# Recurrent stage: the candidate's input share enters its PSUM bank by a product of TensorE

## The chip, the core and the metric

The kernel runs on one core of a Trainium2 chip. The metric is the device time of one execution, in microseconds (us). TensorE appears in the profile as PE (products) and PEld (weight loads), VectorE as DVE, ScalarE as ACT, GpSimd as POOL; a "q" behind an engine's name is its sequencer.

## The reference, cut to what matters

The program is a chain of eight residual blocks over x (8 batches of 256 tokens, 128 features). The third is the recurrent one that the change touches. It walks over the 256 tokens of all 8 batches at once, one step a token, and each step needs the state of the step before:

```
def step(h, x_t):                                  # h: 8 x 128
    score = tanh([h, enc] @ W_att) @ V_att         # enc: 64 context rows of each batch
    attn = softmax(score)
    context = attn @ enc
    gz, gr, gh = split([x_t, context] @ Wi + b)    # input share + context share
    rz, rr, rh = split(h @ Uh)                     # state share
    z, r = sigmoid(gz + rz), sigmoid(gr + rr)
    hh = tanh(gh + r * rh)                         # the candidate
    return z * h + (1 - z) * hh
x = x + the states of all steps
```

The other seven blocks (slot attention, top heads, switch experts, six transformer layers, a top-2 block, a gated block, a quantised linear one) stand before and behind it and are not changed.

## The kernel before, in words

`attentive_gru` (from L1018) has three parts. A preparation makes the input shares `x_t @ Wi + b` of all steps and gates (tile `gx`, gates 0 = z, 1 = r, 2 = candidate) and the context rows times `Wi` (`encw`). Then a hardware loop runs four passes of 64 unrolled steps (L1145, `STEPS_A_PASS`), with a barrier of all engines between passes. A last part adds the states to x.

The order of work is written out by hand for each engine, and semaphores tie the engines together; a wait is named after what it waits for. A step goes round the engines like this. TensorE forms the query (L1185 with the kept part `zh`, L1188 with the new part `part`), VectorE adds it to the encoded context (L1270, two halves), ScalarE takes tanh (L1237, `th`), TensorE makes the scores (L1200), VectorE their minimum (L1274), ScalarE the exponentials (L1239), TensorE turns them (L1209), VectorE copies them (L1278), TensorE makes the three context shares (L1163), VectorE and ScalarE copy these out (L1283, L1241, L1285; `crows`), TensorE turns and adds them into the gates' banks (`turn_part`, L1171), ScalarE takes the gates' tanh (L1244 for r, L1246 for z; a sigmoid is written as half of 1 + tanh), VectorE forms `u` (L1288), `gh` (L1290), `u2` (L1293), `zh` (L1298) and `omz` (L1300), ScalarE the candidate (L1248), VectorE `part` (L1302), and GpSimd the new state (L1255, L1258).

PSUM banks: 0 the query, 5 the r gate, 4 the z gate, 7 the candidate's state share, 6 the candidate's context share, 3 a bank that is never read. Banks 5 and 4 are opened by `input_part` (L1168, an identity product that writes the input share), take the state share (L1194, L1195) and are closed by `turn_part`. Bank 6 is written by `turn_part` alone, and VectorE adds the input share (`gh`).

`keep_busy` (L1157) issues products of a zero tile into the unread bank 3, of 128 to 512 columns. They stand between the real products in TensorE's queue, so that it always has something to do. A step has 13 of them, two of 448 columns before the first wait for `tanh_ready`.

Of the kernel before, what the change touches and what calls it, by code (L numbers as in the profile page):

```python
# [7 lines left out]
ALU = mybir.AluOpType  # L8
# [8 lines left out]
P = 128  # L17
D = 128
B, S = 8, 256
# [998 lines left out]
def attentive_gru(nc, dram, X, psum, cst):  # L1018


    with ExitStack() as ctx:
        def sb(name, shape, dt=F32):
            return ctx.enter_context(nc.sbuf_tensor("g1_" + name, shape, dt))
# [19 lines left out]
        attn, attnT, shares = sb("attn", [P, C]), sb("attnT", [P, B + 32]), sb("shares", [P, B])  # L1043
        crows = sb("crows", [P, 3, D])
        wa_half = sb("wa_half", [P, D])
        gh, kept, tr, tz, u, u2, cand, omz, zh, part = (sb(n, [P, B]) for n in ("gh", "kept", "tr", "tz", "u", "u2", "cand", "omz", "zh", "part"))
        still = sb("still", [P, 512], BF16)

        with engines_pass(nc) as (block, sig):
            @block.sync  # L1050
            def _(sp):
                for dst, src in ((wa, "G1_wa"), (wi, "G1_wi"), (ctxT, "ctxT"), (uh, "G1_uh"), (bias, "G1_bias"),
                                 (vcol, "G1_v"), (pick, "c_pick")):
                    sp.dma_start(dst[:], dram[src]).then_inc(sig["loads"], 16)
                sp.dma_start(h[:, 0, :], dram["embT"]).then_inc(sig["loads"], 16)
# [89 lines left out]
        with nc.Fori(0, S // STEPS_A_PASS) as group:  # L1145


            with engines_pass(nc) as (block, sig):
                def gx(gate, s):
                    return GX[:, gate, :, ds(group * STEPS_A_PASS + s, 1)].rearrange("p b a -> p (b a)")  # L1150

                @block.tensor
                def _(pe):
                    def keep_busy(bank, cols, n=1):

                        for _ in range(n):
                            pe.matmul(psum[:, bank, 0:cols], cst["ident_bf"][:], still[:, 0:cols], start=True, stop=True)  # L1157

                    def context_part(gate, bank, ready):


                        for p in range(PAIRS):
                            last = pe.matmul(psum[32 * p:32 * p + 32, bank, 0:D], attnT[:, 2 * p:2 * p + 32],  # L1163
                                             encw[:, p, gate, :], start=True, stop=True)
                        last.then_inc(sig[ready], 1)

                    def input_part(gate, bank, s):
                        pe.matmul(psum[:, bank, 0:B], cst["ident"][:], gx(gate, s), start=True, stop=False)  # L1168

                    def turn_part(i, bank, ready, start=False):  # L1170
                        pe.matmul(psum[:, bank, 0:B], crows[:, i, :], shares[:], start=start, stop=True)\  # L1171
                          .then_inc(sig[ready], 1)

                    keep_busy(3, 512, 18)
                    input_part(1, 5, 0)
                    input_part(0, 4, 0)
                    for s in range(STEPS_A_PASS):
                        hs = h[:, s % 2, :]

                        if s == 0:  # L1180
                            pe.matmul(psum[:, 0, 0:B], wa[:, 0, :], hs, start=True, stop=True)\
                                .then_inc(sig["query_ready"], 1)
                        else:
                            pe.wait_ge(sig["kept_part_ready"], s)
                            pe.matmul(psum[:, 0, 0:B], wa_half[:], zh[:], start=True, stop=False)  # L1185
                            keep_busy(3, 256)
                            pe.wait_ge(sig["new_part_ready"], s)
                            pe.matmul(psum[:, 0, 0:B], wa[:, 0, :], part[:], start=False, stop=True)\  # L1188
                                .then_inc(sig["query_ready"], 1)
                            keep_busy(3, 256)  # L1190
                            pe.wait_ge(sig["state_ready"], s)
                        pe.matmul(psum[:, 7, 0:B], uh[:, 2, :], hs, start=True, stop=True)\
                          .then_inc(sig["state_products_ready"], 1)
                        pe.matmul(psum[:, 5, 0:B], uh[:, 1, :], hs, start=False, stop=False)  # L1194
                        pe.matmul(psum[:, 4, 0:B], uh[:, 0, :], hs, start=False, stop=False)  # L1195
                        keep_busy(3, 448, 2)
                        for i in range(2):
                            pe.wait_ge(sig["tanh_ready"], 2 * s + i + 1)
                            for p in range(PAIRS):
                                last = pe.matmul(psum[32 * p:32 * p + 32, 1, 0:C], vneg[:, i, :], th[:, i, p, :],  # L1200
                                                 start=i == 0, stop=i == 1)
                            if i == 0:
                                keep_busy(3, 320)
                        last.then_inc(sig["scores_ready"], 1)
                        keep_busy(3, 512, 3)

                        pe.wait_ge(sig["exp_ready"], s + 1)
                        for i in range(2):
                            last = pe.matmul(psum[C * i:C * i + C, 2, 0:B], attn[:], pick[:, i, :], start=True, stop=True)  # L1209
                        last.then_inc(sig["attn_turned"], 1)  # L1210
                        keep_busy(3, 384, 2)
                        pe.wait_ge(sig["attnT_ready"], s + 1)
                        context_part(1, 3, "context_r_ready")
                        context_part(2, 1, "context_h_ready")
                        context_part(0, 2, "context_z_ready")
                        pe.wait_ge(sig["shares_ready"], s + 1)
                        pe.wait_ge(sig["context_r_taken"], s + 1)
                        turn_part(0, 5, "gate_r_ready")
                        pe.wait_ge(sig["context_h_taken"], s + 1)
                        turn_part(1, 6, "context_h_turned", start=True)  # L1220
                        keep_busy(3, 192)
                        pe.wait_ge(sig["context_z_taken"], s + 1)
                        turn_part(2, 4, "gate_z_ready")
                        keep_busy(3, 512)
                        if s + 1 < STEPS_A_PASS:
                            pe.wait_ge(sig["tanh_r_ready"], s + 1)
                            input_part(1, 5, s + 1)
                            keep_busy(3, 128)
                            pe.wait_ge(sig["tanh_z_ready"], s + 1)
                            input_part(0, 4, s + 1)  # L1230
# [32 lines left out]
                def _(dve):  # L1263
                    steps = Steps(dve, sig["vector_steps"])

                    for s in range(STEPS_A_PASS):
                        dve.wait_ge(sig["query_ready"], s + 1)
                        query = psum[:, 0, 0:B].rearrange("p (b i) -> p i b", i=2)
                        for i in range(2):
# [16 lines left out]
                        dve.wait_ge(sig["tanh_r_ready"], s + 1)  # L1286
                        dve.wait_ge(sig["state_products_ready"], s + 1)
                        dve.scalar_tensor_tensor(u[:], tr[:], 1.0, psum[:, 7, 0:B], ALU.add, ALU.mult).then_inc(sig["reset_ready"], 1)  # L1288
                        dve.wait_ge(sig["context_h_turned"], s + 1)
                        dve.tensor_tensor(gh[:], psum[:, 6, 0:B], gx(2, s), ALU.add).then_inc(sig["candidate_part_ready"], 1)  # L1290
                        dve.wait_ge(sig["reset_ready"], s + 1)
                        dve.wait_ge(sig["candidate_part_ready"], s + 1)
                        dve.scalar_tensor_tensor(u2[:], u[:], 0.5, gh[:], ALU.mult, ALU.add)\  # L1293
                            .then_inc(sig["candidate_input_ready"], 1)
                        dve.wait_ge(sig["tanh_z_ready"], s + 1)
                        if s >= 1:
# [2338 lines left out]


PHASES = [slot_attention, top_heads, attentive_gru, switch_experts, dit_layers, top2_block, glu_block, ternary_linear]


# [126 lines left out]
```

## Time and profile before

| | us |
|---|---|
| median of 3 runs | 5760.1 |
| lowest, highest | 5753.37, 5780.07 |
| the profiled execution's own time | 5762.91 |
| its span, from the first to the last instruction | 5761.1 |
| busy: PE 4907.7 (85%), DVE 2920.8 (51%), ACT 2109.4 (37%), POOL 585.3 (10%) | |
| the steps of the recurrent stage | from about 446 to 2235 |

Busy time is a sum over instructions. In the recurrent stage most of what PE does is `keep_busy` (the costliest group of the page, 1018.9 us), so a busy PE doesn't mean that PE sets the time there. "PEclk" is the granted TensorE clock as a share of its upper level: 1.00 is 2.4 GHz, 0.50 is 1.2 GHz.

### The profile page before, as it was taken

How to read it: one execution, taken by the hardware profiler on the slowest of the kernel's cores; microseconds unless marked ns; L12 is line 12 of the kernel's file. 1: busy time of each engine (PE TensorE's matmuls, PEld its weight loads, DVE VectorE, ACT ScalarE, POOL GpSimd, SP SyncE). 2: the span in 40 equal slices, each digit the busy share in tenths (PEclk: the TensorE clock that was granted, in tenths of full speed). 3: DMA queues.
4: the chain of work that ended last, by engine and by line, in shares of the span. 5: the costliest groups of instructions: out<-in, count | busy, mean ns of one | idle time of the engine just before them, and what ended most of it. 6: DMA issues, size and time to landing. Idle time of an engine off the chain costs nothing. (4 is left out here: it accounts for less than half of the span.)

```text
span 5761.1 us, 115322 instructions
## 1 busy us (share of the span) xinstructions
PE 4907.7 (85%) x46515; PEld 3114.7 (54%) x46515; DVE 2920.8 (51%) x9818; ACT 2109.4 (37%) x4155; POOL 585.3 (10%) x1312
## 2 busy tenths in 40 slices
PE   4389999999999996588989888898869897788784
PEld 3256666666666664355545555455534574555563
DVE  5634444444444443477666777677636323334343
ACT  2223222222222221166656666566534332122221
POOL 3300000000000002211111111111110000000000
PEclk7689899898998997699999999999979798898896
DMA  0010000000000001100000000000000001000000
GB/s 24 7 32 2 2 2 2 2 2 2 2 2 2 2 2 50 54 6 4 9 4 9 4 5 5 7 8 4 6 38 1 1 1 41 1 1 1 1 1 9
DMA packets 33174, 51.08 MB, mean 9 GB/s; under 512 B 8596, under 2 KB 24118, under 8 KB 32000
## 3 DMA queue, kind: packets, MB, share of 16 engines
q1 hardware_dynamic: 29312, 39.67, 2.1%
q8 instruction: 383, 6.28, 0.4%
q10 hardware_dynamic: 2304, 2.11, 0.1%
q0 software_dynamic: 1024, 1.78, 0.1%
q14 instruction: 151, 1.24, 0.1%
HBM read 39.03 MB, written 4.19 MB: 8 GB/s over the span
## 5 line engine op out<-in xcount | busy, mean ns | idle before, releaser
L1157 PE MATMUL psum<-g_still,ident_bf 128*128 128x512 bf16 (+6 forms) x3388 | 1018.9, 359 | 19.1 <-issue 17.5
L2277 DVE TENSOR_REDUCE l_m<-psum 128x2 bf16<-128x512 f32 x768 | 503.8, 693 | 164.8 <-PE psum L1881 161.7
L1157 PEld LDWEIGHTS psum<-g_still,ident_bf 128*128 128x128 bf16 x3388 | 409.1, 139 | 144.1 <-issue 84.6
L2153 ACT ACTIVATE l_probs<-psum,l_mcol 128x1024 f32<-128x1024 f32 x384 | 406.7, 1110 | 175.5 <-PE psum L1919 175.5
L1881 PE MATMUL psum<-l_kb,l_qmb 32*128 32x256 bf16 x1536 | 299.0, 276 | 70.6 <-DVE l_m L2277 52.0
L1237 ACT ACTIVATE g_th<-g_pre 128x256 f32<-128x256 f32 x512 | 192.2, 418 | 348.8 <-DVE g_pre L1270 348.8
L1919 PE MATMUL psum<-l_qm,l_keys 32*128 32x256 f32 x3072 | 268.3, 422 | 14.6 <-issue 14.6
L1270 DVE TENSOR_TENSOR g_pre<-g_encp,psum 128x256 f32<-128x256 f32 x512 | 192.9, 418 | 168.4 <-PE psum L1188 120.9
L2164 ACT COPY l_heads_out<-psum 128x256 f32<-128x256 f32 (+1 forms) x292 | 130.3, 446 | 367.6 <-PE psum L1945 184.8
L1945 PE MATMUL psum<-l_probs,l_v 128*32 128x256 f32 x3072 | 222.5, 410 | 46.2 <-DVE l_o L2317 28.7
L2277 DVE TENSOR_REDUCE l_cm<-psum 128x4 bf16<-128x256 f32 x400 | 166.3, 428 | 178.2 <-PE psum L1881 178.0
L1274 DVE TENSOR_REDUCE g_smin<-psum 128x1 f32<-128x64 f32 x256 | 57.6, 225 | 372.7 <-PE psum L1200 372.7
L1171 PEld LDWEIGHTS psum<-g_shares,g_crows 128*128 128x128 f32 x1536 | 197.4, 190 | 79.1 <-issue 79.1
L1919 PEld LDWEIGHTS psum<-l_qm,l_keys 32*128 32x128 f32 x3072 | 183.1, 194 | 104.0 <-issue 95.4
L1171 PE MATMUL psum<-g_shares,g_crows 128*128 128x8 f32 x1536 | 213.3, 245 | 17.4
L1241 ACT COPY g_crows<-psum 128x128 f32<-128x128 f32 x256 | 68.3, 267 | 426.6 <-PE psum L1163 426.6
L1163 PE MATMUL psum<-g_encw,g_attnT 128*32 128x128 f32 x6144 | 223.1, 279 | 0.0
L1255 POOL TENSOR_SCALAR g_kept<-g_zh 128x8 f32<-128x8 f32 x256 | 59.6, 233 | 1543.0 <-DVE g_zh L1298 1543.0
L1881 PEld LDWEIGHTS psum<-l_kb,l_qmb 32*128 32x128 bf16 x1536 | 112.6, 94 | 180.7 <-DVE l_m L2277 82.7
L1163 PEld LDWEIGHTS psum<-g_encw,g_attnT 128*32 128x32 f32 x6144 | 153.6, 110 | 84.8 <-DVE g_attnT L1278 84.5
L1239 ACT ACTIVATE g_attn<-psum,g_smin 128x64 f32<-128x64 f32 x256 | 80.8, 316 | 323.7 <-DVE g_smin L1274 323.7
L3407 ACT ACTIVATE l_probs<-psum 128x1024 f32<-128x1024 f32 x80 | 82.0, 1025 | 310.0 <-PE psum L3234 229.6
(571 smaller groups left out, 10138.6 us busy)
## 6 DMA issues: line engine op xcount, KB each, us to landing
s_w<-in_S_w SPq DMA_DIRECT2D x16, 256.0 KB, 5.0
f_w<-in_F_w SPq DMA_DIRECT2D x2, 2048.0 KB, 12.3
l_wf<-in_L_W SPq DMA_DIRECT2D x7, 576.0 KB, 3.7
l_w<-in_L_W SPq DMA_DIRECT2D x1, 3072.0 KB, 10.4
l_wc<-in_L_W SPq DMA_DIRECT2D x7, 384.0 KB, 2.9
l_nw<-in_L_nw SPq DMA_DIRECT2D x1, 2304.0 KB, 7.9
l_wa<-in_L_W SPq DMA_DIRECT2D x7, 320.0 KB, 2.7
h_w<-in_H_W ACTq DMA_DIRECT2D x16, 129.0 KB, 3.0
```

The costliest lines, as they stand in the source:

```text
L1157: pe.matmul(psum[:, bank, 0:cols], cst["ident_bf"][:], still[:, 0:cols], start=True, stop=True)
L1163: last = pe.matmul(psum[32 * p:32 * p + 32, bank, 0:D], attnT[:, 2 * p:2 * p + 32], encw[:, p, gate, :], start=True, stop=True)
L1171: pe.matmul(psum[:, bank, 0:B], crows[:, i, :], shares[:], start=start, stop=True)\
L1237: act.activation(th[:, i, :, :], pre[:, i, :, :], ACT.Tanh).then_inc(sig["tanh_ready"], 1)
L1270: dve.tensor_tensor(pre[:, i, :, :], encp[:, i, :, :], query[:, i, :].unsqueeze(2).to_broadcast([P, PAIRS, C]), ALU.add)\
L1881: last = pe.matmul(psum[:, bank, x.width * t:x.width * (t + 1)], queries, far_keys, start=True, stop=True)
L1919: last = pe.matmul(psum[:, g, S * part:S * part + S], keys[group(g), s.buf, x.j % 2, S * x.b + P * part:S * x.b + P * part + P], qm[group( ...
L1945: last = pe.matmul(psum[group(g), VALUES, 0:S], v[:, s.buf, 2 * x.b + part, GROUP * g + x.j, :], probs[:, u % 2, part, S * g:S * g + S], s ...
L2153: act.activation(probs[:, u % 2, chunk, :].rearrange("p (g n) -> p g n", g=GROUP), psum[:, 0:GROUP, S * chunk:S * chunk + S], ACT.Exp, bia ...
L2164: act.copy(heads_out[:, u % 2, 0:cols], psum[:, VALUES, 0:cols]).then_inc(sig["values_copied"], 1)
L2277: dve.tensor_reduce(place, psum[:, c.bank(("max", u, g)), 0:x.tiles * x.width] .rearrange("p (t k) -> p t k", t=x.tiles), AX.X, ALU.min)\
L3407: act.activation(probs[:, u % 2, c, :, :].rearrange("p h q -> p (h q)"), psum[:, bank:bank + 2, :].rearrange("p a q -> p (a q)"), ACT.Exp, ...
```

## The change

`input_part` now opens bank 6 as well: a product of the identity with the candidate's input share, behind the state products of each step. It stands where the second of the two `keep_busy` of 448 columns stood. Before it PE waits until VectorE has read bank 6 in the step before (`candidate_input_ready`). `turn_part` then adds the context share to it, and VectorE's addition `gh` is gone: `u2` reads bank 6 itself.

```diff
-        gh, kept, tr, tz, u, u2, cand, omz, zh, part = (sb(n, [P, B]) for n in (...))
+        kept, tr, tz, u, u2, cand, omz, zh, part = (sb(n, [P, B]) for n in (...))
...
-                    def turn_part(i, bank, ready, start=False):
-                        pe.matmul(psum[:, bank, 0:B], crows[:, i, :], shares[:], start=start, stop=True)\
+                    def turn_part(i, bank, ready):
+                        pe.matmul(psum[:, bank, 0:B], crows[:, i, :], shares[:], start=False, stop=True)\
                           .then_inc(sig[ready], 1)
...
-                        keep_busy(3, 448, 2)
+                        keep_busy(3, 448)
+                        if s >= 1:
+                            pe.wait_ge(sig["candidate_input_ready"], s)
+                        input_part(2, 6, s)
                         for i in range(2):
                             pe.wait_ge(sig["tanh_ready"], 2 * s + i + 1)
...
                         pe.wait_ge(sig["context_h_taken"], s + 1)
-                        turn_part(1, 6, "context_h_turned", start=True)
+                        turn_part(1, 6, "gate_h_ready")
                         keep_busy(3, 192)
...
-                        dve.wait_ge(sig["context_h_turned"], s + 1)
-                        dve.tensor_tensor(gh[:], psum[:, 6, 0:B], gx(2, s), ALU.add).then_inc(sig["candidate_part_ready"], 1)
+                        dve.wait_ge(sig["gate_h_ready"], s + 1)
                         dve.wait_ge(sig["reset_ready"], s + 1)
-                        dve.wait_ge(sig["candidate_part_ready"], s + 1)
-                        dve.scalar_tensor_tensor(u2[:], u[:], 0.5, gh[:], ALU.mult, ALU.add)\
+                        dve.scalar_tensor_tensor(u2[:], u[:], 0.5, psum[:, 6, 0:B], ALU.mult, ALU.add)\
                             .then_inc(sig["candidate_input_ready"], 1)
```

VectorE's queue around the candidate, in any step, before (`g_u` stands for both `u` and `u2`; ISA is a small instruction that works out the address of a step's slice of `gx`):

```order
L1288 SCALAR_TENSOR_TENSOR g_u<-g_tr,psum 128x8 [waits state_products_ready,tanh_r_ready]
L1290 ISA [waits context_h_turned]
L1290 TENSOR_TENSOR g_gh<-psum,g_gx 128x8
L1293 SCALAR_TENSOR_TENSOR g_u<-g_u,g_gh 128x8 [waits candidate_part_ready,reset_ready]
L1298 SCALAR_TENSOR_TENSOR g_zh<-g_tz,g_h 128x8 [waits state_ready,tanh_z_ready]
L1300 TENSOR_SCALAR g_omz<-g_tz 128x8
L1302 TENSOR_TENSOR g_part<-g_omz,g_cand 128x8 [waits candidate_ready,vector_steps]
```

The same place with the change:

```order
L1291 SCALAR_TENSOR_TENSOR g_u<-g_tr,psum 128x8 [waits state_products_ready,tanh_r_ready]
L1294 SCALAR_TENSOR_TENSOR g_u<-g_u,psum 128x8 [waits reset_ready,gate_h_ready]
L1299 SCALAR_TENSOR_TENSOR g_zh<-g_tz,g_h 128x8 [waits state_ready,tanh_z_ready]
L1301 TENSOR_SCALAR g_omz<-g_tz 128x8
L1303 TENSOR_TENSOR g_part<-g_omz,g_cand 128x8 [waits candidate_ready,vector_steps]
```

Two rows are gone between `u` and `u2`; the rest keeps its order.

TensorE's queue from the kept part's product to the first scores, before:

```order
L1185 MATMUL psum<-g_zh,g_wa_half 128x8 [waits kept_part_ready]
L1157 MATMUL psum<-g_still,ident_bf 128x256
L1188 MATMUL psum<-g_part,g_wa 128x8 [waits new_part_ready]
L1157 MATMUL psum<-g_still,ident_bf 128x256
L1192 MATMUL psum<-g_h,g_uh 128x8 [waits state_ready]
L1194 MATMUL psum<-g_h,g_uh 128x8
L1195 MATMUL psum<-g_h,g_uh 128x8
L1157 MATMUL psum<-g_still,ident_bf 128x448 x2
L1200 MATMUL psum<-g_th,g_vneg 32x64 [waits tanh_ready]
```

And with the change:

```order
L1188 MATMUL psum<-g_part,g_wa 128x8 [waits new_part_ready]
L1157 MATMUL psum<-g_still,ident_bf 128x256
L1192 MATMUL psum<-g_h,g_uh 128x8 [waits state_ready]
L1194 MATMUL psum<-g_h,g_uh 128x8
L1195 MATMUL psum<-g_h,g_uh 128x8
L1157 MATMUL psum<-g_still,ident_bf 128x448
L1168 ISA [waits candidate_input_ready]
L1168 MATMUL psum<-g_gx,ident 128x8
L1203 MATMUL psum<-g_th,g_vneg 32x64 [waits tanh_ready]
```

One product of 448 columns has made room for an address instruction and a product of 8 columns, both ahead of the wait for `tanh_ready`.

## Rows read from the trace of the kernel before

**Rows 1.** The page: the granted clock in 40 slices of the span.
```profile
PEclk7689899898998997699999999999979798898896
```
**Rows 2.** L1302 (x is its count), from each pass's first to its last: length, clock.
```profile
453.30:886.70 433.40, 10.54 (x63) 0.91 0.01 2
905.38:1336.90 431.52, 10.54 (x63) 0.91 0.01 2
1355.89:1787.50 431.61, 10.54 (x63) 0.91 0.01 2
1804.58:2234.60 430.02, 10.54 (x63) 0.91 0.01 2
```
**Rows 3.** Stretches, two neighbouring steps: length, busy of PE, PEld, DVE, ACT, POOL, then PEclk.
```profile
1214.64:1220.98 6.34, 6.27 (x79) 4.32 (x79) 3.07 (x16) 1.90 (x7) 0.65 (x4) 1.00 0.00 0
1220.98:1228.70 7.72, 7.65 (x79) 4.54 (x79) 3.04 (x15) 1.90 (x7) 0.62 (x4) 0.78 0.01 2
```
**Rows 4.** Stretches, cut where the granted clock changes; columns as in rows 3.
```profile
1205.14:1222.19 17.05, 16.85 (x210) 12.16 (x210) 8.56 (x43) 4.75 (x19) 1.90 (x9) 1.00 0.01 2
1222.20:1225.61 3.41, 3.41 (x26) 1.00 (x27) 0.61 (x3) 0.94 (x3) 0.00 (x0) 0.52 0.00 0
...
1242.68:1246.09 3.41, 3.41 (x27) 1.09 (x27) 0.53 (x3) 0.85 (x3) 0.00 (x0) 0.52 0.00 0
1263.16:1266.57 3.41, 3.41 (x28) 1.12 (x26) 0.48 (x3) 0.80 (x3) 0.00 (x0) 0.52 0.02 5
...
1276.81:1280.22 3.41, 3.41 (x26) 1.27 (x25) 0.83 (x4) 1.06 (x3) 0.00 (x0) 0.52 0.00 0
```
**Rows 5.** Timeline, end of a fast step: start, us, engine, line; idle before in brackets.
```profile
1213.73 0.16 DVE L1288 SCALAR_TENSOR_TENSOR g_u<-g_tr,psum 128x8 f32<-128x8 f32 x1 [0.31 <-ACT g_tr L1244]
1213.86 0.17 DVE L1290 TENSOR_TENSOR g_gh<-psum,g_gx 128x8 f32<-128x8 f32 x1
1213.99 0.18 ACT L1246 ACTIVATE g_tz<-psum 128x8 f32<-128x8 f32 x1 [0.29 <-PE psum L1171]
1214.03 0.28 PE L1168 MATMUL psum<-g_gx,ident 128*128 x2
1214.13 0.17 DVE L1293 SCALAR_TENSOR_TENSOR g_u<-g_u,g_gh 128x8 f32<-128x8 f32 x1
1214.17 0.22 PE L1157 MATMUL psum<-g_still,ident_bf 128*128 128x128 bf16 x1
1214.32 0.16 DVE L1300 TENSOR_SCALAR g_omz<-g_tz 128x8 f32<-128x8 f32 x1
1214.33 0.21 ACT L1248 ACTIVATE g_cand<-g_u 128x8 f32<-128x8 f32 x1 [0.15 <-DVE g_u L1293]
1214.64 0.17 DVE L1302 TENSOR_TENSOR g_part<-g_omz,g_cand 128x8 f32<-128x8 f32 x1 [0.16 <-ACT g_cand L1248]
1214.78 0.27 PE L1157 MATMUL psum<-g_still,ident_bf 128*128 128x256 bf16 x1
1214.86 0.30 PEld L1188 LDWEIGHTS psum<-g_part,g_wa 128*128 128x128 f32 x2
1214.88 0.37 PE L1188 MATMUL psum<-g_part,g_wa 128*128 128x8 f32 x2
```
**Rows 6.** Timeline, start of a fast step, same columns.
```profile
1209.41 0.75 ACT L1237 ACTIVATE g_th<-g_pre 128x256 f32<-128x256 f32 x2 [1.20 <-DVE g_pre L1270]
1209.58 0.54 PE L1157 MATMUL psum<-g_still,ident_bf 128*128 128x448 bf16 x2
1210.04 0.16 PEld L1200 LDWEIGHTS psum<-g_th,g_vneg 128*32 128x32 f32 x8 [0.37 <-ACT g_th L1237]
```
**Rows 7.** Timeline, start of a slow step, same columns.
```profile
1201.69 0.75 ACT L1237 ACTIVATE g_th<-g_pre 128x256 f32<-128x256 f32 x2 [1.20 <-DVE g_pre L1270]
1201.85 0.91 PE L1157 MATMUL psum<-g_still,ident_bf 128*128 128x448 bf16 x2
1202.69 0.20 PEld L1200 LDWEIGHTS psum<-g_th,g_vneg 128*32 128x32 f32 x8 [0.73 <-ACT g_th L1237]
```

More of the change, by code:

```diff
@@ L1045, in attentive_gru @@
         wa_half = sb("wa_half", [P, D])
-        gh, kept, tr, tz, u, u2, cand, omz, zh, part = (sb(n, [P, B]) for n in ("gh", "kept", "tr", "tz", "u", "u2", "cand", "omz", "zh", "part"))
+        kept, tr, tz, u, u2, cand, omz, zh, part = (sb(n, [P, B]) for n in ("kept", "tr", "tz", "u", "u2", "cand", "omz", "zh", "part"))
         still = sb("still", [P, 512], BF16)
```

## The prediction

> **What bounds the kernel now.** I read the clock line of the page first, then the stage's passes, then two neighbouring steps, the clock between them, and last the timeline of one step of each kind. The change touches only the recurrent stage, some 1790 of 5761 us. There the granted clock is near full but not full [rows 1], 0.91 in all four passes [rows 2]. From a pass's first L1302 to its last there are 63 steps; the four lengths add up to 433.40 + 431.52 + 431.61 + 430.02 = 1726.55 us, over 252 steps 6.85 us each. Yet no common step takes 6.85: neighbours take 6.34 us at clock 1.00 and 7.72 us at 0.78 [rows 3]. A slow step costs 7.72 - 6.33 = 1.39 more, so the share of slow steps is (6.85 - 6.33) / 1.39 = 0.37.
>
> The slow steps hold one stretch of 3.41 us in which the clock is at its lower level, 1.2 GHz; between them it is at 2.4 GHz [rows 4]. The starts of these stretches are what the forecast hangs on: 1222.20, 1242.68, 1263.16, 1276.81, so 20.48, 20.48 and 13.65 us apart. Two fast steps and a slow one take 20.4, one fast and one slow 14.1. The spacings are 3 x 6.83 and 2 x 6.83: neither 6.33 nor 7.72, but what the mean step takes. So I read it as a beat. The fall always comes at the same place of a step (here 1.2 to 1.5 us behind L1302), fast steps run ahead of a beat of 6.83 us until their thin place meets the fall, and the slow step throws them back. A step's mean is then set by the beat, and the length of a fast step only decides how often a slow one is needed.
>
> **The change on the path of a fast step.** Without `gh`, `u2` waits for `u` alone. Now `gh` ends at 1213.86 + 0.17 = 1214.03 and `u2` starts at 1214.13, 0.10 later; `u` ends at 1213.73 + 0.16 = 1213.89 [rows 5]. With the same 0.10 `u2` starts at 1213.99, 0.14 sooner; with the 0.03 that separates `u2` from the candidate behind it, the shortest such wait in these rows, it would be 0.21. I take 0.14, since this is again an instruction with two waits whose last one is late. The candidate follows 0.03 behind `u2`, at 1214.19, just free of `tz`, which ends at 1214.17 and would allow 0.16 at most; `part` follows the candidate by 0.10 and has `omz` in time. So `part` is 0.14 sooner.
>
> PE gives less on. L1188's weight load starts 0.05 behind `part`'s end, at 1214.86. It can't start before the filler product ahead of it has, at 1214.78, so it moves by 0.08 [rows 5]. The filler of 256 columns holds the array until 1214.88, so the first of L1188's two products stays; the second comes sooner, because its load no longer follows a late one. The pair L1168, whose first load was early behind a filler, spans 0.28 where L1188 spans 0.37: 0.09 [rows 5]. Both readings agree, and I take 0.08: a fast step goes from 6.33 to 6.25. The bounds are 0 (PE is the limit after all) and 0.14. The kept part's product and the gates' input shares hang on `tz`, which doesn't move.
>
> **The Trainium skill** speaks against a part of this ("VectorE: DVE Perf Modes", the section on the TRN2 errata): an operand in PSUM has a larger fixed cost for VectorE than one in SBUF, 120 cycles against 58. `u2` would then be some 0.06 us longer (an estimate from that page), `part` only 0.08 sooner and the step's gain about the same. The trace doesn't bear the rule out at this size: `u`, which reads PSUM, takes 0.16, `u2`, which reads SBUF, 0.17 [rows 5].
>
> **What PE gets and loses.** Each of 256 steps loses a product of 448 columns and gains an address instruction and a product pair of 8 columns, behind the state products. In a fast step PE waits there 0.37 us for `th` [rows 6]; the pair holds PE from 1214.03 to the next filler at 1214.17, 0.14 us [rows 5], and the filler that went took half of 0.54 or somewhat less, so nothing is late. The address instruction waits for the last step's `u2`, long past; behind it stand the scores of L1200. If this cover were gone it would cost 0.1 us a step. In a slow step the first scores come at 1202.69, 0.58 behind the tanh of the first half (1201.69 + 0.42), against 0.21 in a fast one (1209.41 + 0.42 to 1210.04), since two fillers take 0.91 at the low clock [rows 6, 7]. A filler of 448 columns, half of 0.91 at most, gives way to a pair of about 2 x 0.14: I take 0.10 off a slow step, bounds 0 and 0.37. It then costs 1.29 more than a fast one.
>
> **The sum.** Without the beat: 252 x 0.08 = 20 us, and 0.37 x 252 = 93 slow steps x 0.10 = 9 us, together 29. With the beat almost none of it is left: 6.85 = 6.25 + share x 1.29 gives a share of 0.465 in place of 0.37, that is 117 slow steps in place of 93, and the granted clock of the passes goes from 0.91 to 1 - 0.5 x 0.465 x 3.41 / 6.85 = 0.88 to 0.90. What can be kept is at the ends of a pass, before the first fall: three to five fast steps in each of four passes x 0.08, 1.3 us. Against the profiled execution: 5762.9 - 1.3 = 5761.6; it lies 2.8 over the median of the runs, so the forecast is 5759. A difference of 0.5% (29 us), to 5731 or 5789, is about what a measurement of this kernel tells from no change.
>
> **Rivals.**
> A, the gain gets through. The falls stay as they are, 0.37 of the steps, and every step is shorter: 5760 - 29 = 5731; with 0.14 in place of 0.08 it is 5716. For it speaks that the path through `gh` really ends the wait at L1302. Against it: the spacing of the falls isn't made of step lengths [rows 4]. The Trainium skill ("TensorE: Matmul & The Clock Gate", the section on why this matters for your kernels) would side with A: it says the clock drops when TensorE lies idle in a long gap between matmuls, and there is none here before or after. By that page the loop wouldn't fall at all. The trace doesn't agree: PE is busy 6.27 of 6.34 us in a fast step and the falls come all the same [rows 3, 4].
> B, the change doesn't shorten a step: PE's queue from L1168 to L1188 is already full, or the longer wait form takes the 0.14. Then 5760, told from the forecast only by fast steps that still take 6.33.
> C, slower: the missing 448 columns make the clock fall oftener than the beat asks. Place: the stretch from L1171 to L1200, where only fillers have many columns. At a share of 0.465 it is even; each 0.01 more costs 252 x 0.0129 = 3.3 us, and 0.5% is reached at 0.55. With two of three steps slow the mean is 6.25 + 0.667 x 1.29 = 7.11, 0.26 x 252 = 66 us more: 5826. For it: the falls come where PE has little but small products, and this makes it thinner. Against it: a slow step throws the steps back by more than a fast one gains on the beat (7.54 - 6.83 = 0.71 against 0.58), so two in a row aren't needed.
>
> **How the numbers follow.** The forecast 0.62, A 0.15, B 0.11, C 0.12. A splits at 5731, so faster by over 0.5% gets 0.08; C lies mostly beyond 0.5% but reaches down to the forecast, slower 0.10; the rest, 0.82, is within 0.5%. The range takes in A's whole gain with 0.08 and C up to a share of about 0.52: 5729 to 5782.
>
> **What would show it.** The row of `gh` is gone, the load of L1188 starts right at the filler's start, and fast steps take 6.25 (right) or 6.33 (B). The mean of 63 steps stays at 6.83 to 6.87 and the pass's clock drops to about 0.89 (the beat), or the mean falls to 6.74 at 0.91 (A), or rises over 6.95 at 0.87 or less (C). The spacing of the falls should stay at multiples of 6.83 with 13.65 oftener than 20.48. The forecast is wrong if the mean step moves by over 0.1 us either way, or if a stage outside the loop moves.

## The result, and the profile after

The change makes the kernel slower: 6496.33 us (median of 4 runs, 6451.95 to 6516.32) against 5759.69 us, ratio 1.1255, 95% interval [1.1194, 1.1315]. The forecast was 5759 us, range 5729 to 5782. The profiled execution took 6509.2 us, 746 more than the one of before. Of the 50 executions of the kernel before that stand behind this document one took 6838 us, at a granted clock of 0.63; why isn't known, and no ratio here uses it.

The page's clock line shows where, beside [rows 1]: the recurrent stage, slices 4 to 18 of 40, has the lower clock nearly throughout; behind it the line reads much as before.

```profile
PEclk7685555555655555556799999999998889888886
```

L1303 (L1302 before) from each pass's first to its last, the answer to [rows 2] (length, VectorE's busy time and count, granted clock):

```profile
452.36:1075.06 622.70, 11.35 (x63) 0.53 0.00 1
1092.81:1700.43 607.62, 11.30 (x63) 0.55 0.01 1
1717.91:2344.77 626.86, 11.37 (x63) 0.53 0.01 1
2362.37:2986.43 624.06, 11.35 (x63) 0.53 0.00 1
```

Together 2481.24 us over 252 steps: 9.85 us a step, 3.00 more than before. 2481.24 - 1726.55 = 755 us covers the whole difference of 746. The two kinds of step that the others lie between (columns as in [rows 3]):

```profile
452.38:458.50 6.12, 5.89 (x78) 4.44 (x78) 3.00 (x15) 1.85 (x7) 0.59 (x3) 1.00 0.02 4
477.73:488.08 10.35, 10.02 (x80) 7.38 (x80) 2.99 (x16) 1.78 (x7) 0.63 (x3) 0.50 0.01 2
```

A fast step is shorter than before and shorter than forecast, 6.12 us. But only 4 of the 252 are fast, while 182 take over 10 us: the common step runs at 1.2 GHz from end to end and takes 10.35. In the kernel before, 86 of the stage's 92 stretches at the lower clock ended after 3.41 us, as in [rows 4]. Now 24 of 48 do, and the others last up to 119 us (the clock changes some 0.13 us behind the bounds shown here and in [rows 4], hence 0.98 and 0.52):

```profile
459.94:558.92 98.98, 95.64 (x747) 69.38 (x758) 28.46 (x134) 17.20 (x67) 5.64 (x27) 0.50 0.00 1
558.93:562.33 3.40, 3.40 (x37) 3.16 (x37) 1.72 (x8) 1.31 (x5) 0.63 (x3) 0.98 0.00 0
562.34:565.74 3.40, 3.07 (x29) 1.34 (x33) 0.91 (x5) 0.31 (x1) 0.00 (x0) 0.52 0.02 5
...
569.17:678.38 109.21, 105.54 (x824) 76.64 (x834) 31.40 (x148) 18.91 (x74) 6.27 (x30) 0.50 0.01 1
```

The fall at 459.94 comes 1.3 us behind an L1303 (at 458.64), the place where it came before. What differs is what PE issues behind it. PE's rows of the first 3.4 us behind a fall, in the kernel before:

```profile
1201.85 0.91 PE L1157 MATMUL psum<-g_still,ident_bf 128*128 128x448 bf16 x2
1202.69 0.44 PE L1200 MATMUL psum<-g_th,g_vneg 128*32 128x64 f32 x8
1203.07 0.45 PE L1157 MATMUL psum<-g_still,ident_bf 128*128 128x320 bf16 x1
1203.44 0.44 PE L1200 MATMUL psum<-g_th,g_vneg 128*32 128x64 f32 x8
1203.82 1.46 PE L1157 MATMUL psum<-g_still,ident_bf 128*128 128x512 bf16 x3
```

and with the change (one product of 512 columns is missing from the trace: three stand in the queue and three weight loads in the trace, but two products, behind a gap of 0.33 us put down to "issue"):

```profile
459.90 0.40 PE L1157 MATMUL psum<-g_still,ident_bf 128*128 128x448 bf16 x1
460.10 0.43 PE L1168 MATMUL psum<-g_gx,ident 128*128 x2
460.46 0.44 PE L1203 MATMUL psum<-g_th,g_vneg 128*32 128x64 f32 x8
460.83 0.45 PE L1157 MATMUL psum<-g_still,ident_bf 128*128 128x320 bf16 x1
461.21 0.44 PE L1203 MATMUL psum<-g_th,g_vneg 128*32 128x64 f32 x8
461.99 1.06 PE L1157 MATMUL psum<-g_still,ident_bf 128*128 128x512 bf16 x2 [0.33 <-issue]
```

Before, six fillers with 2752 columns; now five with 2304, and in the place of the sixth a product pair that holds PE for some 0.3 us with 8 columns. Before, the clock rose behind this; now it didn't.

The place of the fall matters as well. The stretch from 562.34, which ended after 3.4 us, began 2.1 us behind its L1303 (at 560.28); the long one from 569.17 began 1.4 us behind its own (at 567.81). It is so all through the trace: the 23 falls within 1.6 us of an L1303 each kept the clock low for 23.9 us or more, and of the 25 that came 1.8 us or more behind one, 24 ended after 3.41 us. Behind a later fall PE is past the product pair, and its stretch takes in the two fillers of 384 columns and the first context products (L1163).

Why the fast step is 6.12, the end of one and the start of another (columns as in [rows 5]):

```profile
1672.52 0.16 DVE L1291 SCALAR_TENSOR_TENSOR g_u<-g_tr,psum 128x8 f32<-128x8 f32 x1 [0.32 <-ACT g_tr L1247]
1672.79 0.16 DVE L1294 SCALAR_TENSOR_TENSOR g_u<-g_u,psum 128x8 f32<-128x8 f32 x1
1673.56 0.27 PE L1157 MATMUL psum<-g_still,ident_bf 128*128 128x256 bf16 x1
1673.56 0.30 PEld L1188 LDWEIGHTS psum<-g_part,g_wa 128*128 128x128 f32 x2
1673.67 0.28 PE L1188 MATMUL psum<-g_part,g_wa 128*128 128x8 f32 x2
```
```profile
1668.32 0.75 ACT L1240 ACTIVATE g_th<-g_pre 128x256 f32<-128x256 f32 x2 [1.26 <-DVE g_pre L1273]
1668.43 0.35 PE L1157 MATMUL psum<-g_still,ident_bf 128*128 128x448 bf16 x1
1668.62 0.28 PE L1168 MATMUL psum<-g_gx,ident 128*128 x2
1668.83 0.16 PEld L1203 LDWEIGHTS psum<-g_th,g_vneg 128*32 128x32 f32 x8
```

`u2` now starts 0.27 behind `u` (0.40 before), L1188's load starts with the filler ahead of it, and its pair spans 0.28 in place of 0.37: the forecast's 0.08 to 0.09. Beside it, the scores' load follows the tanh of the first half by 0.51 from start to start, where it was 0.63 [rows 6]. That 0.12 is the filler's: it had not stood under a cover.

### The profile page after: what moved, and what is told of

It is laid out like the page before. It is cut to its first block and busy times, and to the rows that moved or that the text cites. A ratio compares the mean times of both kernels' runs of the same rounds, so it can differ in the third digit from the quotient of the medians.

```text
span 6507.4 us, 115279 instructions
## 1 busy us (share of the span) xinstructions
PE 5580.1 (86%) x46479; PEld 3748.5 (58%) x46771; DVE 2907.1 (45%) x9562; ACT 2081.8 (32%) x4155; POOL 581.9 (9%) x1312
## 3 DMA queue, kind: packets, MB, share of 16 engines
q10 hardware_dynamic: 2304, 2.11, 0.1%
## 5 line engine op out<-in xcount | busy, mean ns | idle before, releaser
L1157 PE MATMUL psum<-g_still,ident_bf 128*128 128x512 bf16 (+6 forms) x2872 | 1191.2, 456 | 104.6 <-issue 102.6
L1157 PEld LDWEIGHTS psum<-g_still,ident_bf 128*128 128x128 bf16 x3132 | 548.5, 190 | 192.2 <-issue 177.0
L1168 PEld LDWEIGHTS psum<-g_gx,ident 128*128 128x128 f32 x1536 | 403.1, 288 | 30.2
L1171 PEld LDWEIGHTS psum<-g_shares,g_crows 128*128 128x128 f32 x1536 | 324.6, 295 | 95.0 <-issue 95.0
L1163 PE MATMUL psum<-g_encw,g_attnT 128*32 128x128 f32 x6144 | 371.3, 408 | 0.0
L1171 PE MATMUL psum<-g_shares,g_crows 128*128 128x8 f32 x1536 | 347.7, 331 | 1.6
L1163 PEld LDWEIGHTS psum<-g_encw,g_attnT 128*32 128x32 f32 x6144 | 246.4, 161 | 171.9 <-DVE g_attnT L1281 157.1
L1168 PE MATMUL psum<-g_gx,ident 128*128 x1536 | 320.0, 294 | 0.0
```

## The experiments

Fifteen kernels ran. Medians in us; the mean steps are worked out from the four passes as above, in the traced execution. That lies within 0.3% of the median, but for "one filler out" (traced 5861, and its four runs are two pairs 200 us apart) and "pair in the wait, one filler" (traced 6329):

| kernel | fillers of 448 ahead of the scores | input product | VectorE's addition | us | mean step |
|---|---|---|---|---|---|
| before | 2 | none | yes | 5760 | 6.85 |
| pair alone | 2 | ahead of the scores, unread | yes | 5831 | 7.11 |
| one filler out | 1 | none | yes | 5951 | 7.29 |
| share left out | 2 | none | no | 5745 | 6.83 |
| share left out, one filler | 1 | none | no | 5925 | 7.56 |
| the same with a plain pair | 1 | unread, no address | no | 6472 | 9.70 |
| filler back | 2 | ahead of the scores | no | 5865 | 7.31 |
| **the change** | 1 | ahead of the scores | no | 6496 | 9.85 |
| pair in the wait | 2 | in the context wait | no | 5746 | 6.83 |
| pair in the wait, one filler | 1 | in the context wait | no | 6265 | 9.14 |

**The filler back** (ratio 1.0167, [1.0150, 1.0184]):

```diff
-                        keep_busy(3, 448)
+                        keep_busy(3, 448, 2)
                         if s >= 1:
                             pe.wait_ge(sig["candidate_input_ready"], s)
                         input_part(2, 6, s)
```

> The change, with the second filler product of 448 columns kept as well (behind it the new input product). Theory F (the missing filler is what keeps the clock low: a low stretch in which it is missing is too thin for the clock to come back): the low clock no longer lasts, granted clock in the passes back to about 0.9, 5680 to 5765 us. Theory L (the shorter step puts the steps on another rhythm, in which a whole step at the low clock repeats itself): the step is as short as in the change or nearly, so still 6300 to 6500 us. Theory I (the new input product with its address instruction, which has few columns, thins the stretch): also still over 6300 us.

It took 5864.87 us. 631 of the 737 us are gone, so the lasting low clock needs the missing filler; 105 us stay, which theory F didn't foresee. Beside single slow steps there are now 25 stretches at the lower clock that last 13.65 us and hold two slow steps in a row, of 9.1 us each, where [rows 3] has one of 7.72. Two such steps and the stretch that they share, columns as in [rows 3]:

```profile
479.01:488.09 9.08, 9.08 (x79) 6.02 (x79) 2.96 (x16) 1.81 (x8) 0.63 (x3) 0.59 0.01 2
488.10:497.26 9.16, 9.09 (x84) 6.42 (x82) 3.01 (x16) 1.85 (x7) 0.63 (x3) 0.66 0.00 0
480.60:494.25 13.65, 13.65 (x103) 8.86 (x101) 3.44 (x16) 2.54 (x10) 0.63 (x3) 0.50 0.01 1
```

Fast steps took 6.32: with two fillers ahead of it the product pair takes back what VectorE's path gives.

**One filler out of the kernel before** (`keep_busy(3, 448, 2)` to `keep_busy(3, 448)` at L1196, nothing else):

> The kernel before, with one filler product of 448 columns in place of two ahead of the first scores, and nothing else changed (VectorE still adds the candidate's input share). Theory F: the passes fall to a clock near 0.55 and common steps take over 10 us, 6300 to 6600 us. Theory I: 5740 to 5765 us, since no product is added. Theory L: 5740 to 5800 us, since the step gets shorter by 0.07 us at most.

The four runs took 5826.65, 5861.47, 6040.06 and 6055.98 us; with that spread no interval is given, but the lowest is 1.2% over the median of before. Fast steps are 6.17, 0.16 shorter: the second filler stood on the path of a fast step. So no theory was right. The missing filler alone costs 67 to 296 us and not 737, and its effect is uneven. Passes of one execution:

```profile
452.93:927.60 474.67, 10.73 (x63) 0.77 0.01 2
...
1437.39:1875.73 438.34, 10.55 (x63) 0.86 0.01 2
```

**The filler moved**, to the wait for the first context copy; bank 0, because bank 3, which the text above calls unread, takes the r gate's context share and VectorE is reading it then:

```diff
                         context_part(0, 2, "context_z_ready")
+                        keep_busy(0, 448)
                         pe.wait_ge(sig["shares_ready"], s + 1)
```

> The change, with the 448 columns that it removed put back in another place: ahead of the wait for the first context copy, where PE waits for VectorE (bank 0, whose reader is done). Theory F with the place not mattering (what counts are columns anywhere in the thin part of a step): few falls or none, 5550 to 5760 us. Theory F with the place mattering (only columns in the stretch just behind a fall bring the clock back): if a fall comes it stays, over 6300 us. Theory L and theory I: over 6300 us.

5779.90 us, ratio 1.0022, [0.9993, 1.0051]: the same as before. The same number of columns elsewhere takes nearly the whole loss away: it is 20 us over the range of theory F with the place not mattering, and against the other two answers. In three of its four passes fast and slow steps alternate, 6.12 and 7.53, for a mean of 6.83; in the first, runs of low steps still come. A stretch at the lower clock, and this filler behind it:

```profile
790.12:793.53 3.41, 3.41 (x27) 1.16 (x26) 0.91 (x5) 0.50 (x2) 0.00 (x0) 0.50 0.02 5
794.42 0.36 PE L1157 MATMUL psum<-g_still,ident_bf 128*128 128x448 bf16 x1
```

The filler stands behind the stretch: over the whole stage, 124 falls, it never comes less than 3.8 us behind one, and 118 of them are over by then. So it doesn't help by adding columns just behind a fall. What the trace shows is that the falls come later in a step, most of them 1.7 to 2.2 us behind L1304 (L1303 in the change), about where the change's own short stretches began; the two that came earliest, 1.5 and 1.6 us behind it, kept the clock low for 38 and 48 us. Why the filler moves the falls is open.

**Both fillers**, the last two edits together:

> The change with both: the second filler of 448 columns kept, and a further one of 448 columns ahead of the wait for the first context copy. Theory F: the thin part of a step is filled from two sides, the clock falls seldom or never, steps take 6.2 us: 1790 - 256 x 0.65 = 1625 us in the stage, total 5570 to 5650 us. The beat of the forecast, if it is a property of the clock alone: the mean step stays at 6.83, 5750 to 5765 us. Theory L: over 6300 us.

5651.94 us, ratio 0.9802, [0.9785, 0.9818]. This is 2 us over theory F's range. The mean step is 6.48, below the 6.83 of the beat, and 25 stretches at the lower clock are left of 92: the beat is not a property of the clock alone.

The next four separate the product pair from the filler and from the shorter path. **The pair alone**, in the kernel before:

```diff
                         keep_busy(3, 448, 2)
+                        pe.matmul(psum[:, 3, 0:B], cst["ident"][:], gx(2, s), start=True, stop=True)
```

> The kernel before, with the identity product of the candidate's input share added behind the two fillers, into the bank that nobody reads; VectorE still adds the share itself. It prices the product pair without the missing filler and without the shorter path. Theory P (the pair and the missing filler both thin the low stretch, and each alone costs little, since the first run of four put them at about +100 and +60 to +290 us): fast steps 6.33 + 0.07 = 6.40 us, since the pair holds PE ahead of L1200; double falls (steps of 9.1 us) as with the filler back, 5840 to 5900 us. Theory V (the pair costs nothing by itself; the shorter path through VectorE shifts the steps against the falls): 5755 to 5785 us.

5830.81 us, ratio 1.0138, [1.0093, 1.0182]: a little under theory P's 5840, and fast steps 6.45, 0.12 longer. **The pair in the wait**:

```diff
-                        keep_busy(3, 448)
-                        if s >= 1:
-                            pe.wait_ge(sig["candidate_input_ready"], s)
-                        input_part(2, 6, s)
+                        keep_busy(3, 448, 2)
...
                         context_part(0, 2, "context_z_ready")
+                        if s >= 1:
+                            pe.wait_ge(sig["candidate_input_ready"], s)
+                        input_part(2, 6, s)
```

> The change with the input product moved out of the queue ahead of L1200 into the wait for the first context copy (where PE is idle 0.23 us in a fast step), and both fillers of 448 columns kept. Theory P: PE's queue behind a fall is that of the kernel before, so the low clock doesn't last; fast steps are 6.33 - 0.08 = 6.25 us; the mean step is again near 6.83, 5745 to 5770 us. Theory V: the shorter path alone makes double falls, 5840 us or more.

5745.71 us, ratio 0.9984, [0.9967, 1.0001], mean step 6.83: theory P. Fast steps 6.31, not 6.25; the pair isn't free in the wait. **The filler in the wait, without the change** (`keep_busy(0, 448)` as above, in the kernel before):

> The kernel before, with one more filler of 448 columns in the wait for the first context copy (bank 0), nothing of the change. It tells what of the 2% of the kernel with both fillers is the filler's. If all: fast steps stay at 6.33, falls in a tenth of the steps, mean 6.45 to 6.50, 5640 to 5670 us. If the change brings part of it: over 5690 us.

5723.54 us, ratio 0.9929, [0.9906, 0.9952]: the second expectation, over 5690. A third of the 2% is this filler's, the rest needs the change beside it. **The pair in the wait, one filler**:

> The change with the input product moved into the wait for the first context copy, and one filler of 448 columns as in the change. Against the change it takes the pair out of the queue ahead of L1200; against the kernel with one filler out it adds the shorter path. Theory P: as the kernel with one filler out, fast steps 6.17 - 0.08 = 6.09 us, falls oftener, no lasting low clock of 10 us steps for most of a pass, 5830 to 6060 us. Theory V: as the change, over 6300 us.

6265.11 us, ratio 1.0858, [1.0815, 1.0902]: between the two. Theory P had the pair thin the stretch behind a fall only; it does harm elsewhere in the step too, if less.

**The share left out**, with two fillers, then with one. Neither has an input product or an addition:

```diff
-                        if s >= 1:
-                            pe.wait_ge(sig["candidate_input_ready"], s)
-                        input_part(2, 6, s)
...
-                        turn_part(1, 6, "gate_h_ready")
+                        turn_part(1, 6, "gate_h_ready", start=True)
```

> Leaves the candidate's input share out of the computation: no addition on VectorE and no product on PE; both fillers of 448 columns stay. It prices the shorter path alone. The forecast's step: fast steps 6.33 - 0.08 = 6.25 us, the mean step still 6.83, 5750 to 5765 us. Theory V (the shorter path alone brings the falls oftener): mean over 7.0, 5820 us or more.

5744.91 us, ratio 0.9978, [0.9936, 1.0021]. This is the forecast's own case, a shorter step and nothing else, and it went nearly as forecast, 5 us under the range and with the interval taking in no change. Passes, and stretches cut at the clock's changes:

```profile
453.01:882.57 429.56, 10.59 (x63) 0.89 0.01 2
899.57:1330.34 430.77, 10.59 (x63) 0.89 0.01 2
```
```profile
460.78:464.20 3.42, 3.42 (x27) 1.22 (x26) 0.50 (x4) 0.80 (x3) 0.00 (x0) 0.52 0.00 0
...
474.45:477.86 3.41, 3.41 (x27) 1.11 (x25) 0.56 (x3) 0.88 (x3) 0.00 (x0) 0.52 0.02 5
...
488.10:491.51 3.41, 3.41 (x26) 1.02 (x27) 0.65 (x3) 0.97 (x3) 0.00 (x0) 0.52 0.00 0
...
508.58:511.99 3.41, 3.41 (x28) 1.17 (x26) 0.50 (x3) 0.82 (x3) 0.00 (x0) 0.52 0.02 5
```

All four passes add up to 1721.84 us, 6.83 a step, though fast steps shrank to 6.20; the clock is 0.89; the falls lie 13.7, 13.7 and 20.5 us apart. In the whole stage 86 spacings are of 13.7 us and 23 of 20.5, where the kernel before had 13 and 68.

> As the last one, with one filler of 448 columns: the shorter path and the missing filler together, without the product pair. Fast steps 6.17 - 0.08 = 6.09 us. Theory T (the missing filler leaves too few columns behind a fall, and what decides is only the filler and the shorter path, since the kernel with the pair moved into a wait took 6265): low steps of over 10 us that repeat, 6150 us or more. Theory P (the pair, wherever it stands, is needed for that): as the kernel with one filler out, 5830 to 6060 us.

5925.46 us (three runs from 5894 to 5926, the fourth 6101), ratio of the three 1.0267, [1.0222, 1.0312]: theory P. Without the pair the missing filler doesn't keep the clock low for most of a pass, shorter path or not: 62 of 112 stretches end after 3.41 us and 46 after 13.7, though one lasts 85. The last three ran because it was open what of the pair does it, and how sharp the bound is. **A plain pair** in its place:

```diff
                         keep_busy(3, 448)
+                        pe.matmul(psum[:, 3, 0:B], cst["ident"][:], hs, start=True, stop=True)
```

> Leaves the candidate's input share out, as the last one of that kind, with one filler of 448 columns, and adds in the pair's place an unread product of the identity with the state, 8 columns in 32-bit floats: no address instruction and no wait. If the product itself, which holds PE for 0.14 us (0.28 at the low clock) with hardly a column, makes the low clock last: as the change, 6400 to 6550 us. If it is the address instruction or the wait: as without the pair, 5890 to 6100 us.

6471.57 us, ratio 1.1205, [1.1158, 1.1253], 546 us over the last kernel, which differs by this line alone. One pass:

```profile
448.46:1050.97 602.51, 11.29 (x63) 0.56 0.01 1
```

So the product alone, without its address instruction or its wait, is enough for the lasting low clock once the filler is missing. **A second filler of 256 columns, and of 128**, in the change (`keep_busy(3, 256)` or `keep_busy(3, 128)` behind `keep_busy(3, 448)`):

> The change with a second filler of 256 columns ahead of the pair (0 in the change, 6496 us; 448 gave 5865 us). If the low clock's lasting goes by a sharp bound: either as 448 (5860 to 5950 us) or as the change. If it is gradual: about 6130 us, on the line between.

> The change with a second filler of 128 columns ahead of the pair. Sharp: one of the two ends (5860 to 5950 us, or 6400 to 6550 us), gradual: about 6310 us.

6112.04 us (1.0573, [1.0541, 1.0604]) and 6259.52 us (1.0833, [1.0757, 1.0910]). With 0, 128, 256 and 448 columns the series is 6496, 6260, 6112, 5865: gradual. Both traces still hold fast steps, single slow ones and runs of low ones; what changes is how many there are of each.

**A version that beats both.** The change with the filler in the wait, and the thin part filled further:

```diff
-                            keep_busy(3, 256)
+                            keep_busy(3, 512)
                             pe.wait_ge(sig["state_ready"], s)
...
-                        keep_busy(3, 192)
+                        keep_busy(3, 256)
...
                         keep_busy(3, 512)
+                        keep_busy(3, 256)
...
-                            keep_busy(3, 128)
+                            keep_busy(3, 256)
```

> The change with the filler moved into the wait for the context copy, and the thin part of a step filled further: 192 to 256 columns, 512 to 512 and 256, 128 to 256 and 256 to 512, all behind products that PE doesn't wait to send. If falls come only where a step is thin, there are none left: fast steps of 6.15 to 6.20 us throughout, clock 0.99 in the passes, 1790 - 252 x (6.85 - 6.18) gives 5580 to 5610 us in total. If the beat is the clock's own, the mean stays at 6.83 and the time at 5760 us.

> The kernel before with the same further fillers (and the one in the wait for the context copy, both of 448 columns kept): what of the last one is not the change's. Fast steps 6.33 to 6.36 us, no falls or few: 5760 - 252 x (6.85 - 6.36) gives 5630 to 5660 us; so the change would be worth some 45 us once the clock holds. If the change is worth nothing even then, both have the same time.

5579.44 us (ratio 0.9686, [0.9655, 0.9717]), and without the change, with both fillers of 448 columns, 5633.10 us (0.9774, [0.9743, 0.9806]). The passes, first with the change, then without:

```profile
453.28:843.26 389.98, 10.59 (x63) 1.00 0.01 2
861.22:1250.99 389.77, 10.59 (x63) 1.00 0.01 2
```
```profile
451.72:851.32 399.60, 10.57 (x63) 1.00 0.01 2
869.87:1269.24 399.37, 10.57 (x63) 1.00 0.01 2
```

No pass has a fall; steps take 6.19 and 6.34. Where the clock holds, the change's shorter step comes through: 252 x 0.15 = 38 of the 46 us between the two traced executions, whose other 8 lie outside these steps. The medians are 54 us apart.

## Why the prediction was wrong

- *What bounds the stage.* Right. The falls and not the path set the mean step, and the kernel with the share left out shows the beat itself: a fast step shorter by 0.13 us, a mean of 6.83 where it was 6.85, 5745 us. But "the fall always comes at the same place of a step" was read off four falls; over all runs it moves, and the place matters.
- *The path.* The mechanism was right, `u2` 0.13 sooner and 0.08 to 0.09 of it passed on through L1188. A fast step gained 0.21: the term for the fillers ahead of the scores was set at nothing ("the filler that went ... nothing is late"), and it was 0.12. I had read the 0.37 in [rows 6] as PE's wait for `th` and so as a cover, but it stands in the row of the weight loads (PEld); the row above it has the fillers in PE through that time. The kernel with one filler out shows a gain of 0.16 by that alone.
- *The step that failed.* "The slow steps hold one stretch of 3.41 us" was taken for fixed, and with it the 1.29 us that a slow step costs. It hung on what PE issues behind a fall, and so on the queue and on the place of the fall in a step. I priced the edit of the queue in a slow step as a gain of 0.10 us of PE time; it also took 448 of 2752 columns from the stretch after which the clock had risen in 86 of 92 cases, and put some 0.3 us of nearly columnless work there. The clock then stayed low for 99 and 109 us, and the mean step was 9.85 us in place of 6.85.
- *Rival C* had the right cause and place and the wrong size. It made falls more frequent, 5826 us for two of three steps, and the stretches behind them no longer; its chance of 0.12 rested on "two in a row aren't needed", which the kernel with the filler back refutes: with all fillers in place and the pair beside them, slow steps come in twos.
- *The sum of parts.* The missing filler alone costs 67 to 296 us in its four runs (191 by the median), the pair alone 71, the path alone nothing; together 737. So 370 to 600 us come only of the combination, and no single edit shows them.
- *The Trainium skill's* rule ("TensorE: Matmul & The Clock Gate", why this matters for your kernels) ties the drop to gaps in which TensorE idles. Here PE's records are busy for 10.02 of 10.35 us in a step at the lower clock all through, so the trace doesn't agree. The rule on operands in PSUM ("VectorE: DVE Perf Modes", TRN2 errata) isn't borne out for 8 columns: `u2` takes 0.16 from PSUM and took 0.17 from SBUF.

That the missing filler and the product pair together make the low clock last is shown: each alone costs far less, the filler's return or the pair's absence ends most of it, and the plain pair brings it back. That they do it through the stretch just behind a fall is the reading of the rows above; the series of fillers changes the whole step with it, and the filler in the wait shows that the stretch can be left as it is and the falls moved instead. Why the kernel with the wait filler gains more together with the change (5652) than without it (5724) is open.

## What to carry to other kernels

Filler products are part of a kernel's timing: before one is removed or traded for a small product, ask what the clock does with what is left, in the stretch behind a fall as well as in the one ahead of it. A granted clock of 0.91 with short, regular falls is a warning that the kernel stands near an edge; first fill the thin places until the clock holds, in waits where PE is idle anyway, and only then shorten the path: in the kernel as it stood a path shorter by 0.13 us a step gave no time that could be told from none. Small changes that each cost little can cost far more together, here 737 us against 138 to 367 for the sum of the parts, so they are to be measured together.

## What the runs showed of the hardware

- A 32-bit product pair of 8 columns keeps PE's records busy and doesn't keep the clock up: beside one filler of 448 columns, with the share left out, such a pair takes the kernel from 5925 to 6472 us and the granted clock of the passes from 0.70 to 0.78 down to 0.53 to 0.56.
- A step wholly at the lower clock takes 10.35 us and is followed by others like it, mostly for 99 or 109 us at a time, with the same instructions that run at 2.4 GHz in 6.12 us elsewhere in the same pass.
- Falls began at a spacing of whole multiples of 6.83 us in the kernel before (85 of 91 spacings) and with the share left out (110 of 114), at fast steps of 6.33 and of 6.20 us alike.
- With the change, the 23 falls of the clock within 1.6 us of an L1303 lasted 23.9 us or more and 24 of the 25 later ones 3.41 us: the same queue, met at another place.
- A filler ahead of a wait isn't free. In [rows 6] the tanh of the first half ends at 1209.83; the two fillers start at 1209.58, and elsewhere in that trace the second of the two starts 0.19 behind the first at 2.4 GHz (1242.63 and 1242.82), so both are through at about 1209.96 (an estimate); the load of the 32-column products starts at 1210.04, when neither holds it any more. One filler less made the fast step 0.16 shorter. What the last 0.08 is wasn't tried.
